# Writing the masked queries with two fused VectorE operations from PSUM, and normalising in the three-operand form, in a cross-attention and mixture-of-experts layer

## The reference, cut to what matters

```python
x = x + attention(layernorm(x), ctx, ctx)      # 16 heads of 16, scores only inside blocks of 64 rows
x = x + ffn(layernorm(x))                      # 8 experts, the best 2 per row, gelu, layernorm of the sum
```

```python
q, k, v = query @ Wq + bq, key @ Wk + bk, value @ Wv + bv
scores  = einsum('bhqd,bhkd->bhqk', q, k) / sqrt(dk) + block_mask
out     = (softmax(scores) @ v) @ Wo + bo
```

## Time and profile before

| | us |
|---|---|
| median of 3 runs (lowest, highest) | 823.22 (821.9, 823.74) |
| the profiled execution | 824.23 |
| its span | 822.4 |
| mean granted TensorE clock | 0.932 of full speed |

### The profile page before, as it was taken

One profiled execution on the slowest core, in us unless ns is written; L12 is line 12 of the kernel. 1 busy time (PEld: TensorE's weight loads), 2 busy tenths in 40 slices (PEclk: granted clock), 3 DMA queues, 4 the chain that ended last, 5 costly groups with the idle time before them and its releaser, 6 DMA issues.

```text
span 822.4 us, 20968 instructions
## 1 busy us (share of the span) xinstructions
PE 720.0 (88%) x6400; PEld 648.0 (79%) x6401; DVE 536.5 (65%) x1182; ACT 363.5 (44%) x657; POOL 441.4 (54%) x584
## 2 busy tenths in 40 slices
PE   4999999999999718599999999999999999999200
PEld 4999999999999514498899999998899898998100
DVE  4889888888888579455555555555555555554295
ACT  2877777777777403122222222222222222222184
POOL 3777787788787407524444444344443444422287
PEclk9999999999999855699999999999999999999655
DMA  4333333333332100111111111111111111110594
GB/s 157 109 108 121 104 121 103 120 104 119 103 121 85 41 7 0 54 38 53 53 51 47 44 49 45 45 51 51 51 51 45 45 51 45 45 38 27 171 304 164
DMA packets 39875, 64.54 MB, mean 78 GB/s; under 512 B 5408, under 2 KB 30240, under 8 KB 39840
## 3 DMA queue, kind: packets, MB, share of 16 engines
q1 hardware_dynamic: 31632, 42.37, 16.0%
q0 software_dynamic: 7488, 20.46, 7.7%
q10 hardware_dynamic: 720, 1.26, 0.5%
HBM read 45.46 MB, written 18.61 MB: 78 GB/s over the span
## 4 chain that ended last, share of the span: by engine, by line
PE 87%; DVE 4%; issue 3%; DMA 2%; POOL 2%; ACT 1%; SPq 0%; ACTq 0%; DVEq 0%; POOLq 0%
PE ps_a L530 25%; PE ps_b L544 25%; PE ps_b L433 7%; PE ps_a L391 4%; PE ps_b L400 4%; PE ps_c L412 4%; PE ps_c L417 3%; PE ps_a L468 3%; PE ps_a L455 2%; PE ps_c L498 2%; PE ps_c L514 2%; PE ps_a L479 1%; PE ps_c L378 1%; PE ps_a L443 1%; DMA w_hi<-y_rows 1%
## 5 line engine op out<-in xcount | busy, mean ns | idle before, releaser
L530 PE MATMUL ps_a<-area,w_hi 128*128 128x256 f16 x1248 | 207.7, 274 | 1.7 <-DVE area L795 1.7
L544 PE MATMUL ps_b<-w_hi,area 128*128 x1248 | 206.4, 273 | 0.0
L1055 POOL DMA_INDIRECT y_rows<-area x78 | 77.9, 999 | 209.4 <-ACT area L940 197.5
L530 PE MATMUL ps_a<-area,w_lo 128*128 128x256 f16 x624 | 170.7, 274 | 0.0
L544 PE MATMUL ps_b<-w_lo,area 128*128 x624 | 170.1, 273 | 0.0
L935 ACT ACTIVATE area<-ps_a 128x512 f32<-128x512 f32 x156 | 93.1, 597 | 142.0 <-PE ps_a L530 142.0
L530 PEld LDWEIGHTS ps_a<-area,w_hi 128*128 x1248 | 122.3, 98 | 16.1 <-issue 2.1
L544 PEld LDWEIGHTS ps_b<-w_hi,area 128*128 128x128 f16 x1248 | 122.1, 98 | 14.1
L793 DVE TENSOR_SCALAR area<-ps_c 128x512 f16<-128x512 f32 x39 | 27.0, 691 | 151.7 <-PE ps_c L514 151.7
L805 DVE SCALAR_TENSOR_TENSOR area<-area 128x512 f16<-128x512 f32 x156 | 108.3, 694 | 5.4
L940 ACT ACTIVATE area<-ps_b 128x512 f32<-128x512 f32 x39 | 23.3, 597 | 181.1 <-PE ps_b L544 181.1
(11 more groups left out here) (129 smaller groups left out, 1250.2 us busy)
## 6 DMA issues: line engine op xcount, KB each, us to landing
area<-weights SPq DMA_DIRECT2D x32, 512.0 KB, 3.3
w_hi<-y_rows SPq DMA_DIRECT2D x32, 256.0 KB, 4.0
resid<-x_in SPq DMA_DIRECT2D x32, 128.0 KB, 2.1
area<-ctx_t SPq DMA_DIRECT2D x32, 128.0 KB, 2.1
xn_rows<-area SPq DMA_DIRECT2D x32, 128.0 KB, 1.7
out<-w_lo SPq DMA_DIRECT2D x16, 256.0 KB, 2.6
area<-xn_rows,area POOLq DMA_INDIRECT x78, 2.8
y_rows<-area POOLq DMA_INDIRECT x78
```

The lines of the kernel that those rows point to most:

```text
L530: mm = pe.matmul(ps_h[:, q, (ic % 2) * SLOTS:(ic % 2 + 1) * SLOTS], w[:, bass.ds(first + (hc * I + ic * P), P)], r[b][:, hc, :], start=(n ...
L544: mm = pe.matmul(ps_y[:, b, v * D:(v + 1) * D], g[b][:, ic, v * P:(v + 1) * P], w[:, bass.ds(first + (EXPERT_COLS + ic * D), D)], start=(n ...
L1055: pool.indirect_dma_start(y_rows[:, :], bass.IndirectOffsetOnAxis(ap=didx[b][:, v:v + 1], axis=0), y_s[b][:, v * D:(v + 1) * D], None).the ...
```

## The change

`q_b` and POOL's L1005 go away. DVE writes `q_m` itself from PSUM, with one `scalar_tensor_tensor` per half h: queries times the mask column (a value per partition), plus the bias already multiplied by the mask, which stands in a small new buffer `bq_m` and is made once, by four 128x2 operations ahead of the loop. Both layernorms are written as `scalar_tensor_tensor`: (row - mean) * deviation, with the deviation no longer a value per partition but a tensor operand, the 128x1 buffer broadcast to 128x256.

```diff
-                    dve.tensor_scalar(xn, resid[:, bass.ds(t, 1), :].rearrange("p a d -> p (a d)"), mv1[b][:, 0:1], rs1[b],
-                                      ALU.subtract, ALU.mult).then_inc(xn_r, 1)
+                    dve.scalar_tensor_tensor(xn, resid[:, bass.ds(t, 1), :].rearrange("p a d -> p (a d)"), mv1[b][:, 0:1],
+                                             rs1[b].to_broadcast([P, D]), ALU.subtract, ALU.mult).then_inc(xn_r, 1)
...
-                    dve.tensor_scalar(xn2, resid[:, bass.ds(t, 1), :].rearrange("p a d -> p (a d)"), mv2[b][:, 0:1], rs2[b],
-                                      ALU.subtract, ALU.mult).then_inc(xn2_r, 1)
+                    dve.scalar_tensor_tensor(xn2, resid[:, bass.ds(t, 1), :].rearrange("p a d -> p (a d)"), mv2[b][:, 0:1],
+                                             rs2[b].to_broadcast([P, D]), ALU.subtract, ALU.mult).then_inc(xn2_r, 1)
...
                     dve.wait_ge(k_ps, t + 1)
-                    since(dve, q_r, t)
-                    dve.tensor_tensor(q_b, ps_q, bq_s.unsqueeze(2).to_broadcast([P, HC, P]), ALU.add).then_inc(qb_r, 1)
+                    for h in range(2):
+                        dve.scalar_tensor_tensor(q_m.rearrange("p c b h q -> p (c b) h q")[:, :, h, :],
+                                                 ps_q.rearrange("p c (b q) -> p (c b) q", b=NB), cst[:, C_MASK + h:C_MASK + h + 1],
+                                                 bq_m[:, h, :].unsqueeze(2).to_broadcast([P, HC * NB, BLOCK]),
+                                                 ALU.mult, ALU.add).then_inc(q_r, 1)
...
             dve.wait_ge(small_in, 16)
+            for h in range(2):
+                for c in range(HC):
+                    dve.tensor_scalar(bq_m[:, h, c * NB:(c + 1) * NB], bq_s[:, c:c + 1].to_broadcast([P, NB]),
+                                      cst[:, C_MASK + h:C_MASK + h + 1], None, ALU.mult).then_inc(bq_r, 1)
+            dve.wait_ge(bq_r, 2 * HC)
...
-                t, half, b = here(j, u, 1)
-                if valid(t):
-                    if isinstance(t, int) and t == 0:
-                        pool.wait_ge(small_in, 16)
-                    pool.wait_ge(qb_r, t + 1)
-                    since(pool, s_ps, t)
-                    pool.tensor_tensor(q_m.rearrange("p c b h q -> p (c b) h q"),
-                                       q_b.rearrange("p c (b q) -> p (c b) q", b=NB).unsqueeze(2).to_broadcast([P, HC * NB, 2, BLOCK]),
-                                       cst[:, C_MASK:C_MASK + 2].unsqueeze(1).unsqueeze(3).to_broadcast([P, HC * NB, 2, BLOCK]),
-                                       ALU.mult).then_inc(q_r, 1)
```

More of the change, by code:

```diff
@@ L126, in program @@
         q_m = carve(HC * 2 * P).rearrange("p (c b h n) -> p c b h n", c=HC, b=NB, h=2)
-        q_b = carve(HC * P).rearrange("p (c n) -> p c n", c=HC)
+        bq_m = carve(2 * HC * NB).rearrange("p (h y) -> p h y", h=2)
         k_bd = carve(HC * 2 * P).rearrange("p (c s n) -> p c s n", c=HC, s=2)
@@ L220, in program @@
             sem(n) for n in ("wv_scaled", "wv_hi_r", "wv_lo_r", "ctx_scaled", "ctx_hi_r", "ctx_lo_r"))
-        q_r, qb_r, k_ps, k_r, v_ps, v_r = (sem(n) for n in ("q_r", "qb_r", "k_ps", "k_r", "v_ps", "v_r"))
+        q_r, bq_r, k_ps, k_r, v_ps, v_r = (sem(n) for n in ("q_r", "bq_r", "k_ps", "k_r", "v_ps", "v_r"))
         s_ps, max_r, sub_r, p_r, pt_ps, pt_r = (sem(n) for n in ("s_ps", "max_r", "sub_r", "p_r", "pt_ps", "pt_r"))
@@ L382, in step @@
                 if valid(t):
-                    pe.wait_ge(q_r, t + 1)
+                    pe.wait_ge(q_r, 2 * (t + 1))
                     pe.wait_ge(k_r, HC * (t + 1))
@@ L407, in step @@
                     pe.wait_ge(xt_r, t + 1)
-                    since(pe, qb_r, t)
+                    since(pe, q_r, 2 * t)
                     since(pe, k_r, HC * t)
```

## The result

The changed kernel takes 879.51 us (median; 871.84 to 880.17), before 823.35; the ratio is 1.0659, with a 95% interval of 1.0607 to 1.0712. The forecast was 876 us, with a range of 855 to 890. The execution profiled here is the quickest of them, 871.84 us with a span of 870.0; it is 47.6 us over the profiled one of before.

A forecast was written before the change was run, and what follows sets the result against it. PE was taken as the bound at 8.23 us a step, with DVE to replace it at 10.08: 48.1 + 1.8 + 3.5 - 0.4 = 53.0 us on 824.23 makes 877.2, as median 876, range 855 to 890.

The forecast's parts named there:

- POOL's long operation moves in front of L651: Attention steps 4 to 29: POOL's 2.13 us subtraction covers both DVE normalisations, so L651 ends 2.2 us later.
- the rival in which half of the steps get by: Attention stage: both normalisations slip in before L1011 in every other step; loss about 27 us, 850 us; chance 0.04.
- Whether L642 is let in ahead of L1011: Between two POOL operations: L651 ends at about 159.65 if let in, about 159.7 if not; 159.65 taken.
- from the release to L651's end: DVE normalisation behind POOL's operation: the three-operand form streams an estimated 0.30 us instead of 0.15.
- The second query operation: Queries on DVE: one operation of pitch 0.33 us becomes two of pitch 0.39, +0.45 us a step.
- The step: Attention stage: DVE's work grows from 7.42 to 10.07 us, over PE's 8.23, so DVE becomes the bound.
- The trips: Five loop trips: register work and a late row load, hidden before, now count 0.7 us each, 3.5 in all.
- The sum: Whole kernel: 48.1 + 1.8 + 3.5 - 0.4 = 53.0 us added to the profiled execution.
- step 3: Attention stage: the first step held up, 2.65 us longer on DVE with 0.84 idle before, so +1.8 us.
- The start: Ahead of the loop: four operations for `bq_m` in DVE's idle time, costed at nothing, at most 0.5 us.
- a clock that stays low for the stage: PE in attention: idling drops its clock from 2.4 to 1.2 GHz, some 210 us longer, 1035 us; chance 0.03.
- The rival on the other side: L642 and L651: the three-operand form isn't held up, PE stays the bound, 823.5 us; chance 0.08.

The follow-up runs named there:

- the queries alone: The changed kernel with both normalisations put back in the two-operand form, only the queries changed: 871.12 us, ratio 1.0579.
- the second profile: The changed kernel run once more, unaltered, for another trace: 876.45 us, ratio 1.0679; its profiled execution took 877.1 us.

## Why the prediction was right

Point by point, against the first profile:

- **POOL's long operation moves in front of L651, and L651 stands still until it is over.** As forecast, in 25 steps; the rival in which half of the steps get by is seen in two, 3 and 29. Whether L642 is let in ahead of L1011 was left open; it is. L651 ends 173.08 - 165.93 = 7.15 us after L588; the forecast had 7.32 (159.65 - 152.33). The trace has the end of L1011 at 2.26 us behind L1006's, where I had put the pushed-back operation at 2.4.
- **0.28 us from the release to L651's end.** The forecast had 0.30, from doubling the 0.15 of the two-operand form. It held, and the run of the queries alone shows the 0.15 again.
- **The second query operation: +0.45.** From L651's end to L676's it is 175.86 - 173.08 = 2.78 us, against 159.75 - 157.42 = 2.33 before: 0.45.
- **The step.** 9.96 us instead of the 10.08 forecast (its own terms add up to 10.07); L1011 is the difference.
- **The trips.** The 20 steps of the loop, from 64.07 to 268.17, take 204.10 us. 20 x 9.96 is 199.2, and 1.25 of the rest is one fall of the clock; 3.65 is left for five trips, 0.73 each. The forecast had 0.7. The first steps of the trips, which the forecast had in mind, hold 2.8 of it, 0.33 to 0.72 each; the rest lies in other steps, the largest part in step 9 (10.30 us).
- **The sum.** L588 of step 30 stands at 307.51, and at 259.16 before: 48.35 us. That is 25 x (9.96 - 8.23) = 43.2, plus 3.65, plus 2 x 1.25 for the two falls, less 0.9 because the stage starts sooner. Behind it 0.75 is given back. The forecast for this execution was +53.0, and +47.6 was measured.

Four terms were off. The step was 0.12 us too long in the forecast, 3.0 us over 25 steps. The first held-up step was 4 and not 3, and 29 got by, so the sum had 3.6 us too much (one step at 1.85 and the 1.8 of step 3). The start was costed at nothing to 0.5 us late; it was 0.9 us early in this execution (and not so in the second profile). And the falls of the clock had been put aside whole: I had weighed a clock that stays low for the stage, 210 us, and not one that falls for a part of one step at a time, each followed by a wait of DVE for PE of 1.2 to 1.6 us: two in one profile, three in the other, and seven in that of the queries alone, where the steps that hold one take 11.0 to 11.6 us and the ordinary ones 9.7 to 9.8. That the median lies so near to the forecast, 879.5 against 876, is in part luck: the errors have opposite signs. Of the first five executions of the changed kernel those with a lower mean clock are the longer ones (871.84 us at 0.931, 875.77 at 0.923, 879.41 to 880.17 at 0.915 to 0.918), which fits more falls. The clock alone doesn't order them, though: in the second set 877.1 us stands at 0.931 and 883.09 at 0.910. Only one execution of each set has a trace, so what makes the rest of the 8 us between the first profile and the median stays open.

The rival on the other side, that the three-operand form isn't held up, fell at the point where the rows had it weakest: L651 stood still for 1.9 us in every one of those steps.

## What to carry to other kernels

A wait that looks like pure loss may be what keeps two engines off each other: before taking it away, look at what moves up behind it and what the other engine does in that stretch. On DVE count how many tensors of an operation lie in SBUF: with two of them (a one-column broadcast counts as one), or with one in the faster two-operand form, it stood still here until POOL's running operation ended, so keep long POOL operations away from such spots, cut them into pieces, or let the small operand come from PSUM.

## What the runs showed of the hardware that I had not expected

- The turn between DVE and POOL can change where an operation ends, even between POOL operations that stand back to back (0.85 instead of 0.67 us a piece), and in both directions: L1011 grew from 2.13 to 2.31 us for L642, and to 2.43 for L651 where that came first by 0.04 us.
- A broadcast of one column in SBUF is enough as the second tensor to hold DVE up (2.34 us), and the same column in PSUM is not (0.47).
- With PE waiting 1.3 to 1.6 us in each step of some 10 us, its granted clock fell to 1.2 GHz now and then; with transposes in the place of the pauses it stayed at 2.4 GHz. The run with the shorter pauses, the queries alone, had seven falls, the changed kernel two and three, and the run with half of L1011 put behind two, so the length of the pause alone doesn't say how often the clock falls.
